# Layer norm between two graph layers: the mean subtraction on GpSimd, the means two chunks ahead

## What is computed

```python
def _layernorm(x, axis=-1, eps=1e-05):
    m = jnp.mean(x, axis=axis, keepdims=True)
    v = jnp.var(x, axis=axis, keepdims=True)
    return (x - m) / jnp.sqrt(v + eps)

x = _layernorm(x + _L0_gnn_ref(x, edge_index, W1, b1, W2, b2))      # edge MLP, segment sum
x = _layernorm(x + _L1_gnn_ref(x, edge_index, W, att_src, att_dst, bias))  # 4-head graph attention
```

## Time and profile before

| | |
|---|---|
| median of 3 runs | 8199.65 us (8195.93 to 8199.77) |
| profiled execution | 8190.21 us, its span 8188.4 us |
| first layer with its set-up | 0 to 3978 us of the span |
| layer norm between the layers, up to the last product's copy | 3978.2 to 4032.5 us |
| second layer and the end | 4032.5 to 8188.4 us |
| busy | TensorE 75%, VectorE 69%, ScalarE 47%, GpSimd 72% |

### The profile page before, as it was taken

One profiled execution on the slowest core, in us unless ns is written; L12 is line 12 of the kernel. 1 busy time (PEld: TensorE's weight loads), 2 busy tenths in 40 slices (PEclk: granted clock), 3 DMA queues, 4 the chain that ended last, 5 costly groups with the idle time before them and its releaser, 6 DMA issues.

```text
span 8188.4 us, 247871 instructions
## 1 busy us (share of the span) xinstructions
PE 6156.6 (75%) x46847; PEld 4656.7 (57%) x46848; DVE 5648.4 (69%) x13519; ACT 3827.1 (47%) x9600; POOL 5909.3 (72%) x6184
## 2 busy tenths in 40 slices
PE   6788788777877878778457777777777777777777
PEld 5555555555555655555345555555555555555556
DVE  5555555555555555555568888888888888888877
ACT  4444444444444444444234444444444444444444
POOL 4777777777777777777477777777777777777770
PEclk8999999999999989999678888888888888888888
DMA  4222222222222222222221111111111111111120
GB/s 111 41 41 41 41 41 41 42 41 41 42 41 41 41 41 41 41 42 41 35 32 32 31 31 31 32 31 32 32 31 32 31 32 30 32 31 31 31 29 17
DMA packets 299582, 306.84 MB, mean 37 GB/s; under 512 B 193033, under 2 KB 196727, under 8 KB 298633
## 3 DMA queue, kind: packets, MB, share of 16 engines
q0 software_dynamic: 197600, 261.23, 18.2%
q1 hardware_dynamic: 99476, 38.71, 2.1%
q10 hardware_dynamic: 2068, 3.20, 0.1%
HBM read 286.38 MB, written 16.30 MB: 37 GB/s over the span
## 4 chain that ended last, share of the span: by engine, by line
POOL 37%; issue 24%; PE 15%; DVE 9%; SPq 6%; DVEq 3%; POOLq 2%; DMA 2%; ACT 2%; ACTq 0%
POOL big L492 37%; PE pu L1090 5%; SPq L377 4%; POOLq L480 2%; DVE Y L793 2%; PE ps L972 1%; PE pu L986 1%; SPq L373 1%; ACT ST L1210 1%; PE ps L1009 1%; PE pu L1020 1%; DMA big<-x_dram,idx 1%; PE ps L1004 1%; DVE ps L764 1%; DVE rowD L769 1%
## 5 line engine op out<-in xcount | busy, mean ns | idle before, releaser
L492 POOL DMA_INDIRECT big<-x_dram,idx x3087 | 2992.0, 969 | 1032.1 <-issue 1012.6
L492 POOL DMA_INDIRECT big<-q_dram,idx x3088 | 2916.3, 944 | 1033.6 <-issue 1028.8
L1090 PE MATMUL pu<-Y,S 128*128 128x265 f32 x7872 | 2426.3, 459 | 724.7 <-issue 518.9
L1090 PEld LDWEIGHTS pu<-Y,S 128*128 128x128 f32 x7872 | 1662.2, 222 | 1111.1 <-issue 808.9
L793 DVE TENSOR_TENSOR Y<-big,ps 128x1040 f32<-128x1040 f32 x984 | 1212.1, 1232 | 214.0 <-PE pu L1090 120.0
L596 DVE TENSOR_TENSOR S<-ps,few 128x1024 f32 x978 | 1197.5, 1224 | 176.2 <-DVE few L591 112.2
L636 DVE TENSOR_TENSOR ps<-ps,rowX 128x512 f32<-128x512 f32 x491 | 343.4, 699 | 1325.8 <-ACT rowX L1221 1323.8
L1210 ACT COPY ST<-ps 128x1024 bf16<-128x1024 bf16 x489 | 494.9, 1012 | 1278.5 <-PE ps L972 1262.6
L986 PE MATMUL pu<-rowX,S 128*128 128x192 bf16 x3936 | 554.1, 267 | 448.0 <-SPq L397 400.5
L1293 ACT COPY ST<-ps 128x1024 bf16<-128x1024 bf16 x490 | 495.8, 1012 | 544.8 <-PE ps L1113 513.8
L986 PEld LDWEIGHTS pu<-rowX,S 128*128 x3936 | 381.4, 99 | 605.4 <-issue 517.3
(11 more groups left out here) (178 smaller groups left out, 8344.8 us busy)
## 6 DMA issues: line engine op xcount, KB each, us to landing
big<-x_dram SPq DMA_DIRECT2D x6272, 0.3 KB
big<-q_dram SPq DMA_DIRECT2D x6144, 0.4 KB
big<-q_dram,idx POOLq DMA_INDIRECT x3088
big<-x_dram,idx POOLq DMA_INDIRECT x3087
rowX<-flag_dram SPq DMA_DIRECT2D x196, 32.0 KB
x_dram<-big SPq DMA_DIRECT2D x7, 483.0 KB, 6.8
idx<-srcT_dram SPq DMA_DIRECT2D x98, 32.0 KB
dstc<-dstT_dram SPq DMA_DIRECT2D x98, 32.0 KB
```

The costliest lines, as they stand in the source:

```text
L492: nc.gpsimd.indirect_dma_start(o, None, x_dram if l else q_dram, bass.IndirectOffsetOnAxis(ap=idx[:, half, t:t + 1], axis=0)).then_inc(gat ...
L1090: last = t_.matmul(bank, Sf[:, t, :], Y[:, t, :], start=(t == 0), stop=(t == 7))
```

## The change

For the norm between the layers alone (`base == 0`), `centre` ends with the scaled sum, which raises a new semaphore `meaned`. VectorE no longer waits there for its own last instruction. GpSimd, between its gathers of the first and the second layer, waits for `meaned` and subtracts, chunk by chunk, and it is now GpSimd that raises `centred`. VectorE makes the means of chunks 0, 1 and 2 first, and from then on those of chunk c + 2 in the round of chunk c, where it made those of chunk c + 1. The norm at the end stays on VectorE.

```diff
+        meaned = sem("ln_meaned")
...
             for l in range(2):
+                if l:
+                    for c in range(NCH):
+                        pool.wait_ge(meaned, c + 1)
+                        y = x0[:, c * BC:(c + 1) * BC, :]
+                        mm = mean[:, c * BC:(c + 1) * BC]
+                        nc.gpsimd.tensor_tensor(y, y, mm.unsqueeze(2).to_broadcast([P, BC, D]), ALU.subtract
+                                                ).then_inc(centred, 1)
...
                 link(v.tensor_reduce(mm, y, AX.X, ALU.add))
+                if base == 0:
+                    v.tensor_scalar(mm, mm, 1.0 / D, None, ALU.mult).then_inc(meaned, 1)
+                    return
                 link(v.tensor_scalar(mm, mm, 1.0 / D, None, ALU.mult))
...
-            centre(chunk_of(x0, 0), 0, 0)
+            for c in range(3):
+                centre(chunk_of(x0, c), c, 0)
             for c in range(NCH):
-                if c + 1 < NCH:
-                    centre(chunk_of(x0, c + 1), c + 1, 0)
+                if 3 <= c + 2 < NCH:
+                    centre(chunk_of(x0, c + 2), c + 2, 0)
                 spreads(c, 0)
```

## The result

Twenty runs of each kernel gave 8185.68 us (8175.45 to 8196.81) after the change and 8200.94 us (8193.56 to 8209.15) before it. The ratio is 0.9982 with a 95% interval of 0.9975 to 0.9989. The change makes the kernel 15 us faster, where 8200.5 us and no visible difference had been forecast; the range, 8190 to 8210 us, does not hold it. The profiled execution took 8184.2 us; the one before took 8190.21, so the pair of profiles shows 6 of the 15 us.

What follows compares the result with a forecast made beforehand. It took TensorE's chain to bound the norm's 6.73 us rounds, the long layers being untouched. +0.87 us at the norm's start and 0 elsewhere, on a median of 8199.65, gave 8200.5 us; range 8190 to 8210 us.

Steps and rivals of the forecast that it cites:

- Part 1: Norm between the layers: seven subtractions of 1.09 us leave VectorE, yet TensorE's chain keeps each round at 6.73 us.
- Part 2: Norm's start: GpSimd takes 2.05 us (1.42 to 3.8) for a subtraction, delaying the first scaling by 0.87 us.
- the prediction's own formula: Norm's start: it lengthens by 2T - 3.23 us, T being one subtraction on GpSimd; +0.87 us forecast.
- the second rival: Norm's start: the first GpSimd subtraction must load its code, some 6 us, giving 8206.6 us; chance 0.08.
- Part 3: GpSimd's queue and ports in the norm: rounds cover the subtractions; if VectorE must wait, the start grows 1.4 us.
- 0 in the rounds, 0 behind them: Norm's rounds and everything after the norm, second layer included: the change adds or saves 0 us there.
- the fourth rival: Second layer's gathers change pace by their new place in GpSimd's program: 5 ns each makes 15 us either way; chance 0.05.
- signs of being wrong: Norm rounds near 5.6 us or above 7 us, or a second layer differing by more than 10 us.
- Faster by over 0.2%: Whole kernel: the gathers' pace changes and gains more than 16 us; chance 0.02.

Runs made afterwards that it cites:

- a1_dve7: The changed kernel with seven one-column memsets added on VectorE, one ahead of each wait for TensorE's products: 8197.19 us, ratio 0.9998 to the kernel before.
- c_sem7: The kernel before, VectorE still subtracting, with seven of VectorE's thirteen priming semaphore increments moved to GpSimd: 8190.99 us, ratio 0.9983.

## Why the prediction was wrong

**In the norm the mechanism held and the cost of a subtraction was too high.** The start was forecast 0.87 us longer and became 0.13 us longer. *Part 1* said that a round is TensorE's chain and stays 6.73 us when VectorE sheds a subtraction: 6.73 us measured. VectorE's wait rose to 2.11 us and not 2.7, because of the ports (below). *Part 2* put a subtraction on GpSimd at 2.05 us between 1.42 and 3.8; the seven took 1.69 us each, 11.8 us in all. By the prediction's own formula that makes the start 2 x 1.69 - 3.23 = +0.15 us longer. That it comes within 0.02 us is partly luck: the first subtraction started 0.1 us sooner than the formula has it, and the second 0.1 us after the first had ended. A first use cost nothing: the first subtraction took 1.69 us like the others, so the second rival, code loading, is out. The ratio to VectorE's 1.09 us is 1.55, below the 1.96 that the Trainium skill (GPSIMD Engine Reference, "Elementwise — side-by-side cycle accounting") gives for 2048 numbers.

**The ports.** *Part 3* left open whether VectorE waits for GpSimd. It does: the mean's step of 0.17 us lasted 0.78 while a subtraction ran, and variance steps lasted 0.77 or 0.78. The Trainium skill (SBUF — State Buffer, "Who interferes with whom") has it that whoever issues first gets the shared ports for the whole instruction and blocks the other, if VectorE runs in a two-port mode; the two waits agree, and which mode the step ran in no trace shows. It cost little: the step of the second mean ended within 0.02 us of the first subtraction's end.

**The step that failed** is the sentence on the forecast's other end, "0 in the rounds, 0 behind them", and with it the fourth rival. The rival had seen that instructions could change place and that thousands of gathers multiply a small change. But it looked at the place of GpSimd's own program and at the gap of 0.30 us between gathers, found nothing for it, and was given 0.05. Neither moves: the gap is 0.30 us in every trace, and seven instructions on GpSimd alone gave 1.0000. What moved is VectorE's program. The change takes seven instructions out of it, which was counted as work (7.6 us) and never as a shift of all that follows. The odd copy of the group loop then steps back in 110 ns in place of 229, and the stream of gathers, put at nothing, became 11 us shorter in the pair of profiles. A second layer that differs by more than 10 us was among the prediction's own signs of being wrong.

**How a step of 0.1 us gives 15 us.** VectorE does not bound the second layer, and its waits for the gathers rose from 291.9 to 355.0 us. What of the gain the traces show passes through GpSimd. Fewer gathers are held by VectorE's two-input operations: the gathers' busy time fell by 11.3 us in this pair of profiles, and over all kernels its mean goes with the number of short copies. That the place causes the gain is shown in both directions (`a1_dve7` takes it away and leaves the subtraction, `c_sem7` gives it without the subtraction) and by two places forecast ahead of their runs. That the stream carries it is shown less firmly. It is unbroken, held gathers become fewer in the very passes whose step is short, and the means agree (9 and 25 us of gathers for 9 and 24 us of time); but single kernels scatter, and the profiled spans alone don't show it for one copy. Why a shorter step makes fewer gathers collide is only argued. One thing that bears on it is seen in the timeline above: a held gather lasts 1.18 us, and with the 0.30 us behind it the next one starts 1.48 us later, which is also the distance from L812 to L819. So a gather caught by the first is followed by one caught by the second. A changed phase between the two engines could break up such pairs; no run changed the phase by itself.

**The chances.** Faster by over 0.2% had 0.02, and with 0.18% the time stays just within 0.2%. But the range ended at 8190 us on that side because it took in the norm and the scatter of the runs shown, and nothing for the second layer. The starting point was not at fault: over twenty runs the kernel before has 8200.94 us where 8199.65 was taken.

## What to carry to other kernels

An edit that removes or adds instructions ahead of a loop that runs long also moves that loop in instruction memory, and this can be worth more than the edit: here 15 us against 0.1. So before a gain of a few tenths of a per cent is credited to an edit, put the removed instructions back as padding in idle time (or take as many out elsewhere) and time that too. A time that comes as forecast is not enough by itself: with one instruction more it did, and the step and the gathers had not moved. And look at the whole span of both traces, line group by line group: the group that changed its mean without a change in its code is where the cause shows.

## What was new about the hardware

- A branch back in VectorE's program took 110 to 134 ns or 222 to 238 ns to the next instruction, by the place of the loop. Borders every 128 instructions explain which step was long and which short at all nine places tried for the group loop, and forecast two of them; spacings from 123 to 155 would have done the same. They don't explain why a short step is 110 ns at one place and 134 at another. In the first layer, whose program on VectorE no run moved, the two copies step back in 134 and 230 ns in all traces. The Trainium skill (Runtime: NRT & Kernel Launch, "Instruction fetch mechanics") speaks of blocks of 256 instructions and of a stall when a taken branch leaves the window held. Blocks of 256 don't fit: copies 118 apart, of 46 instructions each, can't both have a border inside, and in the kernel before both are slow. The traces show 424 instruction fetches' packets before and 423 after, for some 150 steps of the odd copy, so the extra 0.1 us is no fetch from memory of its own.
- A gather issued by GpSimd about 0.1 us into a VectorE operation with two SBUF inputs takes 1.18 us in place of 0.944 and ends 0.82 us after that operation. The Trainium skill (SBUF — State Buffer, "Who interferes with whom") has it that such operations disturb GpSimd's reads of SBUF and did not stall descriptor generation. These gathers read their indices from SBUF (`idx`), so the rows agree with the first half. Against the second they say nothing sure, as no run separates the reading of the indices from the descriptors.
- A subtraction of 128 x 896 numbers (f32) takes 1.69 us on GpSimd and 1.09 us on VectorE, and while it runs a small one-input VectorE step of 0.17 us takes up to 0.78 us.
